# Pair sums of the down weights on POOL, and the low halves of z one chunk later in the first tile

## The reference

```python
y = einsum('bct,bcd->bdt', x, cond_weights[itok])
# ternary weights, one scale per matrix
scale = mean(abs(W)); Wq = scale * clip(round(W / scale), -1, 1)
# an octonion linear layer: 8 parts of the input, 8 parts of the output
M = einsum('jik,jod->koid', S_OCT, Wq); out = einsum('...id,koid->...ko', xp, M)
h = silu(oct(y, w_gate)) * oct(y, w_up)      # 1024 -> 2732
out = x + oct(h, w_down)                     # 2732 -> 1024
```

## Time and profile before

| | us |
|---|---|
| median of 3 runs | 698.95 |
| lowest, highest | 697.36, 699.12 |
| the profiled execution, device time | 700.02 |
| its span, first to last instruction | 698.2 |
| PE busy in the span | 658.9 (94%) |
| DVE busy | 528.3 (76%) |
| ACT busy | 325.7 (47%) |
| POOL busy | 360.8 (52%) |

### The profile page before, as it was taken

One profiled execution on the slowest core, in us unless ns is written; L12 is line 12 of the kernel. 1 busy time (PEld: TensorE's weight loads), 2 busy tenths in 40 slices (PEclk: granted clock), 3 DMA queues, 4 the chain that ended last, 5 costly groups with the idle time before them and its releaser, 6 DMA issues.

```text
span 698.2 us, 17481 instructions
## 1 busy us (share of the span) xinstructions
PE 658.9 (94%) x7174; PEld 605.8 (87%) x7174; DVE 528.3 (76%) x897; ACT 325.7 (47%) x562; POOL 360.8 (52%) x411
## 2 busy tenths in 40 slices
PE   3579989999999999999999999999999999999988
PEld 3468978899999998999999999999999999988986
DVE  1898956867877697777878688776878678787884
ACT  4545665254443536254553545345452544435440
POOL 1200468347646566358555466367653476465553
PEclk9799999999999999999999999999999999999996
DMA  8200003032002200032001310022000300021001
GB/s 334 65 2 1 1 2 127 1 123 65 2 1 87 100 2 2 2 121 65 2 2 36 95 58 2 1 92 96 2 1 4 120 2 1 3 91 32 1 2 61
DMA packets 10578, 31.54 MB, mean 45 GB/s; under 512 B 3330, under 2 KB 3330, under 8 KB 10370
## 3 DMA queue, kind: packets, MB, share of 16 engines
q1 hardware_dynamic: 9906, 28.81, 11.7%
q10 hardware_dynamic: 592, 1.61, 0.7%
HBM read 22.02 MB, written 8.39 MB: 44 GB/s over the span
## 4 chain that ended last, share of the span: by engine, by line
PE 72%; DVE 13%; ACT 7%; issue 4%; POOL 2%; DMA 1%; ACTq 1%; DVEq 0%
PE ps L1154 40%; PE ps L1309 23%; PE ps L1141 4%; PE ps L1162 3%; DVE pu_sb L801 2%; DVE pu_sb L932 2%; ACT z_op L697 2%; DVE pu_sb L965 1%; DVE z_op L910 1%; PE ps L1214 1%; POOL h_pairs L592 1%; ACT h_op L678 1%; DVE odd_gu_sb L801 1%; ACT h_f L683 1%; DMA cond_bd<-in_L_cond_weights_dram 1%
## 5 line engine op out<-in xcount | busy, mean ns | idle before, releaser
L592 POOL TENSOR_TENSOR h_pairs<-h_f 128x256 f32<-128x256 f32 (+2 forms) x128 | 135.4, 1085 | 189.1 <-ACT h_f L683 131.3
L1154 PE MATMUL ps<-y_op,gate_table 128*128 128x256 f16 x1408 | 181.5, 274 | 7.0 <-DVE y_op L894 4.2
L1154 PE MATMUL ps<-y_op,up_table 128*128 128x256 f16 x1408 | 180.9, 274 | 0.2 <-DVE up_table L846 0.2
L1154 PEld LDWEIGHTS ps<-y_op,gate_table 128*128 128x128 f16 x1408 | 137.7, 98 | 24.4 <-DVE y_op L894 4.3
L1154 PEld LDWEIGHTS ps<-y_op,up_table 128*128 128x128 f16 x1408 | 138.2, 98 | 17.1 <-DVE up_table L846 0.7
L503 POOL TENSOR_TENSOR o_sb<-o_sb,wd_sb 128x256 f32<-128x256 f32 (+1 forms) x150 | 87.3, 617 | 91.4 <-DVE wd_sb L1026 90.2
L592 POOL TENSOR_TENSOR z_f<-h_pairs 128x512 f32<-128x512 f32 (+1 forms) x80 | 103.1, 1310 | 33.4 <-DVE z_op L910 31.1
L1162 PE MATMUL ps<-third_table,y_op 128*128 128x170 f16 x1408 | 108.3, 236 | 0.0
L1162 PEld LDWEIGHTS ps<-third_table,y_op 128*128 128x128 f16 x1408 | 104.7, 97 | 0.3
L1309 PE MATMUL ps<-down_u,z_op 128*128 128x256 f16 (+1 forms) x768 | 93.5, 279 | 3.0 <-DVE z_op L910 3.0
L801 DVE TENSOR_TENSOR pu_sb<-ps,q_sb 128x170 f32<-128x170 f32 (+1 forms) x128 | 65.0, 508 | 40.8 <-ACT q_sb L714 16.2
(11 more groups left out here) (98 smaller groups left out, 640.2 us busy)
## 6 DMA issues: line engine op xcount, KB each, us to landing
x_in<-in_x_dram SPq DMA_DIRECT2D x8, 1024.0 KB, 5.2
o_sb<-in_x_dram SPq DMA_DIRECT2D x16, 512.0 KB, 3.5
out_dram<-o_sb SPq DMA_DIRECT2D x15, 512.0 KB, 2.7
h_op<-in_L_ffn_w_gate_dram ACTq DMA_DIRECT2D x3, 512.0 KB, 6.5
h_op<-in_L_ffn_w_up_dram SPq DMA_DIRECT2D x3, 512.0 KB, 7.3
z_op<-in_L_ffn_w_down_dram SPq DMA_DIRECT2D x1, 1536.0 KB, 11.3
out_dram<-o_sb SPq DMA_DIRECT2D x2, 256.0 KB, 2.7
cond_bd<-in_L_cond_weights_dram SPq DMA_DIRECT2D x30, 16.0 KB, 2.9
```

What stands on the lines that cost most here:

```text
L592: return pool.tensor_tensor(dst, a, b, ALU.add if sign > 0 else ALU.subtract)
L1154: mm = pe.matmul(dst, table[m][:, slot, q, :], y_op[:, op, e, :], start=(i == 0 and e == 0), stop=(i == len(terms) - 1 and e == 1))
```

## The change

It has four parts, all in tile 0. (1) POOL gets `pair_down(w)`: the sum and the difference of neighbouring ternary blocks of one window, two operations of 128 x 512 f16, into a new view `pairs_down` that lies in `wd_sb`. Windows 0 and 1 stand ahead of POOL's wait for the finished tables, window 2 between rounds 0 and 1 of z. (2) Each mix on PE takes two terms from `pairs_down` instead of four from `tern_down`, so 8 matmuls instead of 16, and waits for `down_paired`. (3) The z halves of rounds 0, 1, 2 are made behind chunks 9, 10, 11 instead of 8, 9, 10; round 3, which was behind chunk 11, comes behind the last `split_h` and `h_lo`, ahead of `y_hi(1)` on ACT and of `last_round_of_z` on DVE. (4) `mix_down` of tile 0 also waits for the last mix, since it overwrites `wd_sb`.

```diff
-    Z_AFTER_FIRST = {8: 0, 9: 1, 10: 2, 11: 3}
+    Z_AFTER_FIRST = {9: 0, 10: 1, 11: 2}
...
+        pairs_down = wd_sb[:].rearrange("p s k r h o -> p (s k r h o)").bitcast(F16)[:, 0:NQ * raw_n].rearrange(
+            "p (w x j o) -> p w x j o", w=NQ, x=2, j=4)
...
-            ks = range(NR - 2, NR)
+            ks = range(NR - 2 if T > 0 else len(Z_AFTER_FIRST), NR)
...
-                    first = 4 * (h ^ v) + 2 * a
                     sign = f[2 * a] * (1, parity(r1))[a]
                     other = parity(r0) if f[2 * a] == f[2 * a + 1] else -parity(r0)
-                    terms += [(first, sign), (first + 1, sign * other)]
+                    terms.append((0 if other > 0 else 1, 2 * (h ^ v) + a, sign))
...
+            def pair_down(w):
+                pool.wait_ge(tern_ready[2], w + 1)
+                a, b = (tern_down[:, w, i::2, :] for i in range(2))
+                for x in range(2):
+                    signed_add(pairs_down[:, w, x], a, b, parity(x)).then_inc(down_paired, 1)
...
                 if T == 0:
+                    pair_down(0)
+                    pair_down(1)
                     pool.wait_ge(slots_built[1], NQ * NBUILD)
-                    for k in range(4):
+                    round_of_z(T, 0)
+                    pair_down(2)
+                    for k in range(1, 4):
                         round_of_z(T, k)
                     sum_y(1)
                     round_of_z(T, 4)
...
                 split_h(T, NC - 1)
+                ks = list(last_rounds(T))
+                if T == 0:
+                    z_hi(T, ks.pop(0))
                 if T + 1 < NT:
                     y_hi(T + 1)
-                for k in last_rounds(T):
+                for k in ks:
                     z_hi(T, k)
...
+                if T == 0:
+
+                    dve.wait_ge(down_mixed, len(MIXES))
...
                 h_lo(T, NC - 1)
+                ks = list(last_rounds(T))
+                if T == 0:
+                    z_lo(T, ks.pop(0))
                 last_round_of_z(T)
-                for i, k in enumerate(last_rounds(T)):
+                for i, k in enumerate(ks):
                     z_lo(T, k, NR - 2 + i)
...
-                pe.wait_ge(tern_ready[2], w + 1)
+                pe.wait_ge(down_paired, 2 * w + 2)
...
-                    for t, (j, sign) in enumerate(mixes[h, v, r]):
-                        mm = pe.matmul(bank_mix[:, r, :], (ident if sign > 0 else minus_ident)[:], tern_down[:, w, j, :],
-                                       start=(r == 0 and t == 0), stop=(t == 3), skip_group_check=True)
+                    for t, (x, j, sign) in enumerate(mixes[h, v, r]):
+                        mm = pe.matmul(bank_mix[:, r, :], (ident if sign > 0 else minus_ident)[:],
+                                       pairs_down[:, w, x, j, :], start=(r == 0 and t == 0), stop=(t == 1),
+                                       skip_group_check=True)
```

More of the change, by code:

```diff
@@ L394, in build @@
         slots_built = [sem("gate_slots_built"), sem("up_slots_built")]
+        down_paired = sem("down_paired")
         down_mixed = sem("down_mixed")
@@ L470, in build @@
                 for a in range(2):
-                    first = 4 * (h ^ v) + 2 * a
                     sign = f[2 * a] * (1, parity(r1))[a]
                     other = parity(r0) if f[2 * a] == f[2 * a + 1] else -parity(r0)
-                    terms += [(first, sign), (first + 1, sign * other)]
-                mixes[h, v, r] = sorted(terms, key=lambda t: -t[1])
+                    terms.append((0 if other > 0 else 1, 2 * (h ^ v) + a, sign))
+                mixes[h, v, r] = sorted(terms, key=lambda t: -t[2])
         MIXES = [(w, h, v) for w in range(NQ) for h, v in F_SIGN]
```

## The result

| | before | changed |
|---|---|---|
| median of 6 runs each, us | 697.73 | 703.24 |
| lowest, highest | 696.78, 699.12 | 700.87, 704.38 |
| profiled execution: device time, span | 700.02, 698.2 | 700.87, 699.1 |

The account below looks back on a forecast made before the run. Tile 1's start on PE bounds: POOL and DVE make it 3.2 us later, with PE's clock fall 3.8 to 5.6, taken as 4.5. Added to 698.95 this gives 703.4 us; 8-in-10 range 697.6 to 705.4.

Parts of the forecast that it names:

- the term of POOL and DVE: Tile 0 to tile 1: later z halves delay POOL's last stretch, so through POOL and DVE tile 1 starts 3.2 us later.
- What bounds the kernel: Tile 1's start on PE: set by round 2's low half through POOL and DVE, PE's down stage about a microsecond closer.
- Fewer matmuls: Tile 0 mixes on PE: 96 fewer matmuls, 5.4 us of PE time, little on the path; 0.44 us of DVE's wait goes.
- Pair sums: POOL in tile 0: 2.5 us per pair_down, bounds 0.8 and 5 us, costing nothing in the likely case.
- PE's pause: PE ahead of tile 0's window-1 down products: stands about 5.8 us for round 3's low half, instead of 0.94.
- The gain of chunk 8: DVE without z halves behind chunk 8: 2.7 us gained at chunk 9's second half, kept through chunks 9 to 11.
- Round 2's low half: DVE behind chunk 11: takes 1.22 us, done at 109.8 instead of 106.4, so POOL's last stretch starts 3.4 us later.
- The clock's term: PE's pause in down: clock halves, returns 10.2 us later, PE loses 3.2 to 5.1; tile 1 4.5 us later.
- rival B: PE's pause in down: no third clock fall or a shorter one; POOL and DVE bind, +3.2, 702.2 us; chance 0.10.
- Rival A: Last tile on PE: its clock fall fails to come, 5.1 us less, 698.3 us, no change; chance 0.22.
- Rival C: Tile 0: PE's work is the path, z halves done in time, 5.4 us come off whole, 693.5 us; chance 0.08.
- Rival D: Chunks gain more: 3.8 instead of 2.7 at chunk 9, 1.8 more if POOL runs free; about 700.2; chance 0.10.

Follow-up runs that it names:

- pair-sums-only run: Changed kernel with the z halves back behind chunks 8 to 11, keeping pair sums on POOL and half mixes; 697.61 us, ratio 0.9997 to the kernel before.
- the copies late and the y sums early: Half mixes, pair sums, z halves in old places, ACT's down_c copies behind z_hi, POOL's y sums ahead of round 0; ratio 0.9955 to the kernel before.
- the run with the filled pause: Changed kernel plus 88 unused identity matmuls on PE in its pause ahead of tile 0's window-1 down products; 703.57 us, ratio 1.0085 to the kernel before.
- full mixes, copies late, y sums early: Kernel before, no pair sums, with ACT's down_c copies behind z_hi and POOL's tile 1 y sums in idle time ahead of round 0; ratio 0.9949.
- later halves only: Kernel before with the z halves one chunk later, as in the change, full mixes and no pair sums; 703.77 us, ratio 1.0086 to the kernel before.

## Why the prediction was right, and where it was not

The time, 703.24 against 703.4, lies closer than the reasoning deserves, and part of that is luck. Two steps were off and compensated each other: the term of POOL and DVE was 0.8 us too small, and the 1.3 us for the clock were not there. The base was off too: I added 4.5 us to 698.95, and the kernel before has 697.73 over six runs, so the measured difference is 5.2 to 5.5 us.

**Held.** *What bounds the kernel*: tile 1's start follows POOL's round 4 by 9.0 us in both profiles (130.45 - 121.43, 133.86 - 124.83); moving the y sums and moving the halves back both moved the start as this says. *Fewer matmuls*: 0.44 us a mix, and 0.45 us gone from DVE's wait at chunk 6 (0.88 to 0.43). *Pair sums*: 2.26 us for two, where I took 2.5, nearly hidden: 0.2 us of the half mixes' 0.44 went to the collision in the pair-sums-only run. (Window 0's weights are ready five chunks ahead of their mix, not two or three; it changes nothing.) GPSIMD Engine Reference of the Trainium skill (section "4.1 Engine selection") would have kept them off POOL. In the kernel with the copies late and the y sums early they cost 0.75 us of start, by collision and not by their own length. *POOL's last stretch*: 124.83 - 112.79 = 12.0 behind round 3, where I took 12.2. *PE's pause*: 5.87 against 5.8.

**The gain of chunk 8 was mis-sized.** I took 2.7 us at chunk 9's low half. From the fixed point it is (98.34 - 67.30) - (95.59 - 66.70) = 2.15. The missing 0.5 is the part "as much again as POOL no longer runs into DVE's last ternary step": that step took 2.17 us again, for POOL is still in round 0 (to 84.47) when it starts at 83.39. Round 1's pairs, which `pair_down(2)` had pushed there, also ran into chunk 8's product (1.57 us instead of 0.57), which I had not seen; it is off the path, as chunk 9's second half waits for PE. DVE in the kernel before:

```profile
84.43 2.17 DVE L827 SCALAR_TENSOR_TENSOR o_sb<-z_op,small,o_sb 128x1024 f16<-128x1024 f32 x1
...
98.34 1.23 DVE L910 TENSOR_TENSOR z_op<-z_f,z_op 128x1024 f16<-128x1024 f32 x1 [2.74 <-ACT z_op L697]
```

**Round 2's low half was priced too low.** I took 1.22 us "as POOL is idle there". POOL was in round 3's pairs, and it took 1.66. Together the POOL and DVE chain is 4.0 us later, not 3.2.

**The clock's term was not there.** The fall in the pause came as forecast, but it lasted 6.8 us, not the 10.2 of both rows, and cost PE 1.5 (16 products in 3.28 us instead of 1.76). PE's chain ended at 132.9 and DVE's let tile 1 start at 133.86. The 1.3 us that I put on for it are refuted by the run with the filled pause. So the start is 4.0 later by DVE alone, where I had 4.5 by the clock: the mechanism is rival B's, to which I gave 0.10, with a larger DVE term.

**Rival A** (the last tile's clock stays up) came in none of the changed kernel's two profiles as I described it, but in 2 of all 13. There the 32 and 96 matmuls took 3.67 and 5.53 us (full mixes, copies late, y sums early; PE):

```profile
677.33 3.67 PE L1309 MATMUL ps<-down_u,z_op 85*128 85x256 f16 x32 [2.09 <-DVE z_op L910]
680.83 5.53 PE L1309 MATMUL ps<-down_c,h_op 128*128 128x128 f16 x96
```

That is 5.0 us less, near the 5.1 that I priced, but from tile 7's start to the end it saves only 2.6 (83.9 us against 86.5): the chain of waits then ends over DVE's last sums instead of PE. So A was overpriced twofold, and my evidence against it (three runs within 1.8 us) was too thin. There is also a case between that I had not seen: in four profiles, the changed kernel's first among them, the last fall lasted 6.8 us instead of 10.2, and the same stretch took 84.9 to 85.4 us. **Rival C** fell: the pair-sums-only run keeps 0.2 of its 5.4 us. **Rival D** fell: it needed 3.8 us at chunk 9, and 2.15 came; of its second half a part did (POOL's pairs of the short window took 3.67 us for four instead of 4.57, where D had 2.8).

**What stays open.** The start explains 4.0 us; the timed runs say 5.2 (3.8 to 6.5), and 4.6 the second time (2.9 to 6.4). The intervals allow 4.0. The two profiles add up: the changed kernel's is 0.6 us ahead at the fixed point, loses 4.0 to tile 1, gains 0.9 in the tiles behind (one tile of the kernel before is 0.8 longer) and 1.6 in the last tile, where the low clock lasted 6.8 us instead of 10.2; that leaves the 0.9 us between the spans.

The scatter has its causes in rows: the first low stretch ended between 29.4 and 32.2, the clock fell or did not fall behind the pause at 51 us (below; it moves all that follows by 1 to 1.7 us), the low stretch of the last tile had three lengths (0, 6.8 and 10.2 us), and seven tiles in six profiles are 0.8 to 1.1 us longer than 80.02. In each of those seven PE stands 1.13 to 1.42 us ahead of one transpose of the third window, for DVE's product; in the kernel before ACT had first waited 0.88 us for POOL's `z_f` (at 264.31). Why POOL was late there I did not find. PE:

```profile
268.91 0.64 PE L1214 MATMUL ps<-ident_f,pu_sb 128*85 128x128 f32 x4 [1.14 <-DVE pu_sb L965]
```

Each timed run of the experiments has its mean granted clock, and that allows an estimate of what the kernels cost apart from this scatter. Over 73 runs of the kernel before, the time falls by 0.50 us for each 0.001 of the mean clock. The fall in the pause, whose cost is in the start already, takes 6.8 / 2 / 699 = 0.0049 off the mean. With that given back, the changed kernel lies 3.8 and 4.3 us above the line of the kernel before (its two sets of runs), where its start is 4.0 later; with the pause filled, and nothing to give back, it lies 4.1 above, with the start again 4.0 later. The two fastest kernels lie 3.1 and 4.0 us below it, with starts 3.2 and 4.0 earlier. Eleven of the twelve sets of timed runs agree with their start to within 0.6 us; later halves only is the exception (3.9 for a start 4.9 later). So by this estimate nothing of size behind tile 1's start tells the kernels apart, and the 5.2 holds about 1 us of falls of the clock elsewhere. Whether those came by chance or by the later start is open.

## What to carry to other kernels

Find the point at which the edited stage hands over to the next (here PE's first product of tile 1) and walk both chains that lead there, with their distance: here they were 1.3 us apart, so every move had to be weighed on both, and relieving one engine of 5.4 us brought 0.2. Work that needs nothing late (the y sums) does not belong into the stretch that sets the handover; moving it gave 2 us, while moving a step "one chunk later" to make room cost 4. And when a profile's ends scatter by some microseconds, compare from a fixed point ahead of the edit to the handover: that repeated to 0.01 us where the medians scattered by 1.5.

## What the runs showed of the hardware

- The clock of PE came back after about 6.8 us in some profiles and after about 10.2 in others, for the same stretch of the same program (the early fall lasted 6.8 us in the changed kernel's first profile and 10.2 in its second), with PE at work again well before. Nor does a pause decide by its length: the one of 2.09 us in the last tile brought a fall in 11 of the 13 profiles, the one of 2.22 us near 51 us, which left the clock high in the kernel before, in 9 of 13. There the clock is low for some 3.4 us only. Windows of PE in the changed kernel's second profile (busy, then clock):

```profile
50.00:52.00 2.00, 1.14 (x10) 1.00 0.00 0
52.00:54.00 2.00, 2.00 (x13) 0.55 0.03 8
54.00:56.00 2.00, 2.00 (x13) 0.60 0.00 0
```

  In the last tile, from its start to the end, the three lengths of the fall took 83.9 us (none, 2 profiles), 84.9 to 85.4 (6.8 us, 4 profiles) and 86.5 to 86.8 (10.2 us, 7 profiles).

  The fixed point at chunk 5 lies behind the fall near 51 us and takes it out; it is at 66.6 to 67.3 us in the four profiles without that fall and at 68.1 to 68.8 in the nine with it.
- An operation on DVE with SBUF inputs that starts while POOL is in one of its own can take about 1 us longer: `z_lo` 2.29 instead of 1.23, the multiply of a short chunk 1.57 instead of 0.57. SBUF — State Buffer of the Trainium skill (section "SBUF: two separate sides") says that the two take a shared pair of ports by an exclusive lock and that the loser blocks for the whole instruction. The extra 1.0 is near the 1.25 of POOL's 128 x 512 operations, which fits it better than the rows that I had before the change; in the prediction I set that rule aside too early. No run here was made to test the rule by itself.
- POOL adds two 128 x 512 f16 tiles in 1.13 us, little less than f32 ones (1.25).
